# The last scaling of two layer norms, moved from VectorE to ScalarE in thirteen units

## What is computed

```python
x = _layernorm(x + _L0_attn_ref(x, Wqkv, bqkv, Wo, bo))
x = _layernorm(x + _L0_xattn_ref(x, ctx, ctx, Wq, bq, Wk, bk, Wv, bv, gamma, beta))
x = _layernorm(x + _L0_ffn_ref(x, w_router, wi, wo))

def _layernorm(x, axis=-1, eps=1e-05):
    m = jnp.mean(x, axis=axis, keepdims=True)
    v = jnp.var(x, axis=axis, keepdims=True)
    return (x - m) / jnp.sqrt(v + eps)
```

## Time and profile before

| what | value |
|---|---|
| median of 3 runs | 618.51 us (616.61 to 618.95) |
| the profiled execution | 622.54 us |
| its span, first to last instruction | 620.8 us |
| TensorE busy | 516.4 us, 83% |
| VectorE busy | 345.1 us, 56% |
| ScalarE busy | 212.4 us, 34% |
| GpSimd busy | 146.8 us, 24% |
| mean granted TensorE clock | 0.939 |

### The profile page before, as it was taken

How to read it: one execution, slowest core, us unless ns; L and a number is a source line. 1 busy time by engine, 2 the same in 40 slices (tenths; PEclk the granted TensorE clock), 3 DMA queues, 4 the chain that set the end, 5 groups by cost and what they waited for, 6 DMA issues and landing times. The chain is left out here.

```text
span 620.8 us, 12743 instructions
## 1 busy us (share of the span) xinstructions
PE 516.4 (83%) x5028; PEld 400.6 (65%) x5028; DVE 345.1 (56%) x968; ACT 212.4 (34%) x475; POOL 146.8 (24%) x160
## 2 busy tenths in 40 slices
PE   5188696979799989989889879679887999999960
PEld 4156475657567667767667656457677888888850
DVE  3456464646667767777677967674365122243214
ACT  2013253315444544544544624333420110212103
POOL 4000011003004004004104166000213764332330
PEclk9688798979999999999999989799998999999995
DMA  5989917675685585595449566345657734799214
GB/s 167 118 122 140 164 25 124 76 90 69 90 122 92 87 130 86 93 131 79 79 78 148 71 111 187 41 164 172 190 192 256 233 43 54 216 286 277 25 19 139
DMA packets 69383, 77.39 MB, mean 125 GB/s; under 512 B 24094, under 2 KB 62621, under 8 KB 66252
## 3 DMA queue, kind: packets, MB, share of 16 engines
q1 hardware_dynamic: 52456, 37.77, 42.0%
q10 hardware_dynamic: 10724, 33.51, 16.2%
q0 software_dynamic: 6144, 5.29, 5.3%
HBM read 38.74 MB, written 13.74 MB: 85 GB/s over the span
## 5 line engine op out<-in xcount | busy, mean ns | idle before, releaser
L949 DVE TENSOR_REDUCE negm<-nat 128x4 f32<-128x512 f32 (+2 forms) x192 | 120.1, 642 | 86.0 <-PE nat L544 83.3
L768 ACT ACTIVATE probs<-byk 128x512 f32<-128x512 f32 (+1 forms) x192 | 105.5, 564 | 117.2 <-PE byk L544 103.0
L544 PE MATMUL nat<-arena 96*128 96x128 bf16 (+2 forms) x512 | 74.3, 249 | 0.0
L544 PE MATMUL byk<-arena 99*128 99x128 bf16 (+2 forms) x512 | 72.5, 244 | 0.0
L544 PEld LDWEIGHTS nat<-arena 96*128 96x128 bf16 x512 | 47.2, 102 | 16.8 <-issue 3.6
L544 PEld LDWEIGHTS byk<-arena 99*128 99x128 bf16 x512 | 46.2, 100 | 18.1 <-issue 1.4
L540 PE MATMUL nat<-window_q,identb 128*128 128x384 bf16 (+1 forms) x96 | 36.3, 378 | 20.3 <-DMA arena<-parts_k 13.7
L1213 POOL TENSOR_TENSOR resk<-fk,parts_k 128x512 f32<-128x512 f32 x8 | 9.3, 1158 | 160.2 <-ACT fk L709 107.3
L671 PE MATMUL work<-woT,arena 128*128 128x160 f32 x256 | 39.8, 310 | 4.6 <-issue 3.8
L671 PE MATMUL work<-yn_T,arena 128*128 128x160 f32 x256 | 40.6, 313 | 3.4 <-DVE r_s L1124 2.4
L540 PE MATMUL byk<-window_k,identb 128*128 128x384 bf16 (+1 forms) x96 | 34.3, 358 | 10.7 <-DMA arena<-mT 9.9
(11 more groups left out here) (187 smaller groups left out, 887.6 us busy)
## 6 DMA issues: line engine op xcount, KB each, us to landing
arena<-parts_q SPq DMA_DIRECT2D x96, 128.0 KB, 4.8
arena<-parts_k SPq DMA_DIRECT2D x96, 128.0 KB, 5.2
arena<-in_ffn_wi ACTq DMA_DIRECT2D x12, 1024.0 KB, 5.3
arena<-in_ffn_wo ACTq DMA_DIRECT2D x12, 1024.0 KB, 8.7
expert_x<-ranked ACTq DMA_DIRECT2D x4, 650.0 KB, 4.7
xres<-in_x ACTq DMA_DIRECT2D x8, 256.0 KB, 5.7
token_y<-xres SPq DMA_DIRECT2D x8, 256.0 KB, 5.0
xres<-token_y SPq DMA_DIRECT2D x8, 256.0 KB, 3.6
```

The lines of the kernel that those rows point to most:

```text
L544: last = nc.tensor.matmul(bank[:, i * w:(i + 1) * w], lhsT, rhs, start=False, stop=(i == heads - 1), skip_group_check=True)
L768: nc.scalar.activation(dst, src, ACT.Exp, scale=0.25).then_inc(exp_ready, 1)
L949: V.tensor_reduce(dst, src, AX, ALU.max, negate=True).then_inc(nat_free[job % 2], 1)
```

## The change

In the units s0 to s6 and c0 to c5 VectorE stops after the Newton step and one 128x2 instruction, the shift (minus the mean times the root). ScalarE then does both scalings as activations (Identity) with the shift as bias column and the root as scale column. Two new pieces carry them: S3 at 37.9 slots of a self unit (L3 stands at 36.8) and S2 at 38.7 of a cross unit (L2 stands at 37.7). The units s7, c6 and c7 stay as they were. Two waits are added on VectorE, in WO and FQ, so that the rows that ScalarE still reads are not overwritten.

```diff
+SCALED_BY_ACT = {"s": 7, "c": 6}
...
+            if b < SCALED_BY_ACT["s"]:
+                add(n0 + 37.9 - sooner, "S3", k)
...
+            if b < SCALED_BY_ACT["c"]:
+                add(n0 + 38.7, "S2", k)
...
+            def scaled(layer, b, dst_of, ready):
+                act.wait_ge(shifted[layer], b + 1)
+                for t in range(QT):
+                    i = nc.scalar.activation(dst_of(t), r[layer][:, t, :], ACT.Identity, bias=shift[layer][:, t:t + 1], scale=rstd[layer][:, t:t + 1])
+                i.then_inc(ready, 1)
+
+            def S2(k, n, layer, b):
+                scaled("c", b, lambda t: xres[:, b * QT + t, 0:D], x2_ready)
+
+            def S3(k, n, layer, b):
+                scaled("s", b, lambda t: x1[:, b % X1S, t, :], x1_ready)
...
             def FQ(k, n, layer, b):
                 bank = computed(dve, "FQ", k)
                 for name in ("YA", "YB"):
                     emptied(dve, name, k)
+                wait(dve, x2_ready, b)
...
+            def shift_for_act(layer):
+                V.scalar_tensor_tensor(out=shift[layer][:, :], in0=mv[layer][:, :, 0], scalar=-1.0, in1=rstd[layer][:, :], op0=ALU.mult, op1=ALU.mult)\
+                    .then_inc(shifted[layer], 1)
+
...
             def L2(k, n, layer, b):
                 refine("c", 2 * b + 1)
+                if b < SCALED_BY_ACT["c"]:
+                    shift_for_act("c")
+                    return
                 scaled("c", lambda t: xres[:, b * QT + t, 0:D]).then_inc(x2_ready, 1)
 
             def WO(k, n, layer, b):
                 bank = computed(dve, "WO", k)
                 dve.wait_ge(xb_ready, b + 1)
+                wait(dve, x1_ready, b)
...
             def L3(k, n, layer, b):
                 refine("s", b)
+                if b < SCALED_BY_ACT["s"]:
+                    shift_for_act("s")
+                    return
                 scaled("s", lambda t: x1[:, b % X1S, t, :]).then_inc(x1_ready, 1)
```

More of the change, by code:

```diff
@@ L263, in attention_and_experts @@
         newton = sb("newton", [P, QT])
+        shift = {layer: sb(f"shift_{layer}", [P, QT]) for layer in "sc"}
         eps = sb("eps", [P, 1])
@@ L332, in attention_and_experts @@
         x1_ready = sem("x1_ready"); x1b_ready = sem("x1b_ready"); x2_ready = sem("x2_ready")
+        shifted = {layer: sem(f"shifted_{layer}") for layer in "sc"}
         var_ready = {n: sem(f"var_ready_{n}") for n in ("s", "c", "out")}
@@ L869, in _ @@
             walk({"QS": QS, "KS": KS, "KC": KC, "QC": QC, "XC": copy_out("XC", x1_T), "Y2": copy_out("Y2", yn_T, "WO"),
-                  "XR": copy_out("XR", x2_T, "RT"), "MT": MT, "T": T_, "PV": PV, "R1": R1, "R2": R2, "R3": R3, "GC": GC, "XL": XL, "LD": LD, "WL": WL,
+                  "XR": copy_out("XR", x2_T, "RT"), "MT": MT, "T": T_, "PV": PV, "R1": R1, "R2": R2, "R3": R3, "S2": S2, "S3": S3, "GC": GC, "XL": XL, "LD": LD, "WL": WL,
                   "H0": hidden("H0", range(0, 3)), "H2": hidden("H2", range(6, 8)), "FR": FR, "FN": FN})
```

## The result

The changed kernel takes **648.94 us** (median of 4 executions, 642.20 to 652.12) against 618.73 us before: 1.0431 times the time, interval 1.0365 to 1.0497. Measured again, six executions beside 17 of before, it is 646.17 against 621.60, a ratio of 1.0384 [1.0337, 1.0431]. The forecast was 634.4, in a range of 624 to 640. So the direction was right, and the size was too small: 15.9 us were to be added, and 30.2 and 24.6 us were, by these medians. The profiled execution of after took 642.20, the fastest of its four: 19.7 us more than the profiled 622.54 of before.

What follows compares the result with a forecast made beforehand. TensorE, 46.11 of 50 us busy in attention, was taken as the bound. Terms 6.3 + 2.6 + 3.5 - 1.1 + 4.6 = 15.9 us on the median of 618.51 gave 634.4 us, range 624 to 640.

Steps and rivals of the forecast that it cites:

- The sum without the clock: Whole kernel: added waits less the early gain, with no added low-clock stretches, 11.3 us.
- the self units: S3 delays exponentials in s4 to s6, 3.5 us; s1 and s3 gain 1.1 us; s0 and s2 nothing.
- the cross units: S2 on ScalarE delays TensorE: 6.3 us at c0 to c2, 2.6 us at c3 to c5 together.
- the rule weighed there: At c0 to c2: counting the DMA issue at nothing would make each delay 0.9 us less; the prediction counted it.
- The clock: Behind XR's new 2.96 us gaps at c0 to c2, one 1.2 GHz stretch each, 4.6 us; c3 nothing, at most 1.5.
- The early gain of 1.1 us: In s1 and s3 TensorE's waits for VectorE's row maxima and reduction end 0.57 us earlier each, 1.1 us gained.
- The clock stays up: Rival: no low-clock stretches behind the new XR gaps, so 11.3 us added, 629.8 us; chance 0.17.
- A later wait takes it back: Rival: TensorE's 4.74 us wait for the last unit's DMA absorbs up to 4.7 us, 629.7 us; chance 0.13.
- VectorE's relief decides: Rival: S2 and S3 delay nothing and each unit gives back 0.57 us, 7.4 us gained, 611.1 us; chance 0.05.

Runs made afterwards that it cites:

- again: The changed kernel with no edit, run again in six executions beside 17 of the kernel before: 646.17 us, ratio 1.0384 to the kernel before.
- s_only: The changed kernel with only the self units s0 to s6 scaling on ScalarE: 627.05 us, ratio 1.0107 to the kernel before.
- c_only: The changed kernel with only the cross units c0 to c5 scaling on ScalarE: 644.2 us, no interval.
- mt_sp6: The changed kernel with SP instead of ScalarE issuing the row maxima's DMA from unit 6 on: 636.3 us, ratio 1.0235 to the kernel before.
- filler: The changed kernel with TensorE transposing the identity, results unused, while XR of c0 to c3 waits: 637.6 us, ratio 1.0271 to the kernel before.
- s3_late: The changed kernel with only self units scaling on ScalarE, S3 of s4 to s6 behind the exponentials: 619.96 us, ratio 1.0007 to the kernel before.
- s2_first: The changed kernel with S2 at 37.9 slots, ahead of the exponential, maxima's copy and DMA issue: 632.26 us, ratio 1.0187 to the kernel before.
- mended: The changed kernel, all thirteen units, with S2 at 37.9 slots and S3 of s4 to s6 at 40.95: 625.01 us, ratio 1.0086 to the kernel before.

## Why the prediction was right in direction and too low

**Right: the waits.** The sum without the clock was 11.3 us; the rest of again stands 12.4 us above before. That these are so close is in part luck: by s_only and c_only the self units cost 5.3 us in the rest where 2.4 were forecast, and the cross units 8.1 where 8.9 were. At the places themselves the fit is better: XR of c0 to c2 waits for ScalarE's line, 2.89 us against 2.96 forecast; c3's gap is 1.97 against 2.0; the first exponential behind S3 in s4 is 1.44 us late against 1.46. The cause was also right: ScalarE comes to S2 only behind a copy and a DMA issue, and when S2 is put in front of them the gap is 1.24 us. On the rule weighed there, the runs are with the earlier trace rows: taking the issue off ScalarE (mt_sp6) shortened XR's gap by 0.9 us and the kernel by about 9, some of it perhaps not owed to the change. That the issue stops the engine holds for the maxima's, which waits for the copy ahead of it, and not for every issue: in mt_sp6 two others ran beside ScalarE's work. The Trainium skill (DMA: Bandwidth & Descriptors, Issuing engines are not separate DMA queues) calls that issuing time usually small beside the transfer; no run here speaks against the comparison, as after's loads of x take 6.1 us from issue to landing and 0.54 us to issue (medians). But small beside the transfer was not small for the engine that issued.

**Wrong: "The clock", the step "so I take one such stretch for each, 3 x 1.54 = 4.6 us".** That one gap costs one stretch of 3.2 us was read from a single row of before. A gap of the very length that was forecast stood in the same trace, with more than one such stretch behind it:

```profile
132.67 0.50 PE L540 MATMUL byk<-window_k,identb 128*128 128x384 bf16 x1 [2.88 <-DMA arena<-mT]
```

```profile
132.70:138.30 5.60, 5.60 (x24) 4.64 (x25) 2.75 (x6) 0.98 (x2) 1.27 (x1) 0.50 0.25 59
```

In the profile of after, the fastest of its four, it is so: c0, c1 and c2 lose 1.45, 1.59 and 1.60 us. But the same 2.89 us gap is followed in other executions by 6.6 or 10 us at 0.50, and c3's, "nothing" in the prediction, also by a stretch. Take filler's steps at c0 to c3, where the clock stays up, from those of the other profiles: what is left for the clock is 6.2 us in after, 10.7 in again and 12.4 in c_only, where the prediction had 4.6 for the first three and nothing for the fourth. That it is the gap which does it is shown by filler: with ScalarE's delay left as it was, the granted clock behind all four XRs is 1.00 and 7 to 8.5 us are gone by the medians. (The 11.5 us between again and before also hold the low time elsewhere.) This is also why the range was too short at its high end: it held 1.5 us for c3, and nothing for longer stretches.

The rule by which the step chose, one row with the clock down behind 2.51 us and one with it up behind 1.9 us, does not hold in the profiles either, though it gave the right answer for 2.89 us. Behind 2 us the clock fell more often than not, and the row of 2.51 us could as well have shown it up. Of such gaps in all thirteen profiles:

| TensorE's gap | place | followed by 0.50 |
|---|---|---|
| 2.89 to 2.90 us | XR of c0 to c2 | 9 of 9 |
| 2.51 to 2.73 us | Y2 of s7, the place of the earlier trace rows, no filler | 6 of 11 |
| 1.97 to 1.98 us | XR of c0 to c3 | 8 of 11 |
| 1.24 to 1.30 us | XR of c0 to c3 | 1 of 8 |
| 1.10 to 1.14 us | XR of c0 to c3 (filler) | 0 of 4 |
| 0.61 to 0.75 us | XR of c0 to c3 | 0 of 20 |

In after the gap of the earlier trace rows stands so:

```profile
377.35 0.66 PE L491 MATMUL work<-ident,ynat_s 128*128 128x128 f32 x4 [2.52 <-DVEq L1012]
```

```profile
377.40:385.00 7.60, 7.59 (x61) 5.74 (x61) 3.75 (x9) 1.74 (x4) 6.51 (x6) 1.00 0.77 121
```

**Mis-sized: the self units**, 2.4 us net against 5.5 to 6.6 (s_only). s5 and s6 took 1.2 and 1.1 against 1.25 and 1.0. At s4 it was 4.6 against 1.25: the last of the three DMA issues between S3 and the exponential took 2.25 us instead of 0.54 (+1.7), and a slow stretch followed the gap that was left (+1.2). The prediction took the issue's length as unchanged. Why it is long there is open: it was 2.21 in s_only and 0.54 in s3_late, where S3 comes later; in filler it was short at s4, but an issue of 2.1 us stood at s6. One such issue, of 1.8 to 2.25 us, stands at s4, s5 or s6 in six of the seven profiles with S3 at its old place (not in s2_first), and in none of the six others, where the longest is 0.7 us: it goes with S3's place. The slow stretch does not need it: in filler the clock fell at s4 behind a gap of 1.16 us. The early gain of 1.1 us was seen on the spot,

```profile
123.25 0.28 PE L580 MATMUL work<-identb,mp 128*128 128x128 bf16 x2 [0.92 <-DVE mp L979]
```

0.92 in place of 1.75 us, and s3's gap of 0.58 us is gone too, but they were not shown to reach the end: s3_late keeps them and is at 1.0007.

With the measured sizes the sum is 5.3 for the self units and 8.1 for the cross units' waits, 13.4 against a rest of 12.4 in again. For the clock behind XR it is 7 to 8.5 by filler: 20 to 22 us of the 24.6 by the medians of again. The remaining 3 to 4 us are not placed; the slow stretch behind s4 is one candidate.

**The rivals.** "The clock stays up" fell at once, on five stretches at 0.50. "A later wait takes it back" fell too: the wait of 4.74 us for the parts' DMA is still 4.59 us in after, at 409.78. "VectorE's relief decides" was tried in its own terms by s3_late: with nobody delayed, the relief of the self units is worth nothing measurable; for the cross units no kernel without any delay was run. That bears on the Trainium skill's condition for such a move, that VectorE is saturated (Perfetto Trace Analysis, Optimizing Scalar/DVE Operations): with 38.77 us busy of 50 it was not the bound.

**Still open**: why the low clock lasts 3.3 us once and 10 us another time behind equal gaps, why equal gaps of 2.5 and 2.0 us bring it in some executions and not in others, and why one DMA issue is long where S3 stands at its old place. That the longer stretches make up the spread of the executions without a profile is argued from their span and mean clock, not seen in their rows.

## What to carry to other kernels

An instruction given to a less busy engine costs by its place in that engine's order: by what stands in front of it (copies, DMA issues) and by who waits for what comes behind; put it where that engine would wait itself, as s3_late did, and the cost is gone. Where no such place was found, as for S2, a part of it stays (mended, 1.0086). First ask whether the engine relieved is one that TensorE waits for, since otherwise there is nothing to gain. And price an idle gap of TensorE at more than its length, with a spread, when the rows show the lower clock behind such gaps; one row of one execution is not enough, for here equal gaps of 1.3 to 2.5 us went either way. Filling the gaps with useless transposes is then worth a try on the kernel as it stands. Look also for an issue that waits for its own engine's result: what stands behind it waits as well.

## What the hardware showed that was not expected

- Equal gaps, unequal stretches: behind 2.89 us the granted clock was 0.50 for 3.2, 6.6 or 10 us; behind 1.97 us for some 3.4, 6.8 or 10 us or not at all.
- Useless work paid: 220 transposes in nine waits took 0.85% off the kernel before.
- A DMA issue on ScalarE held back what stood behind it when it waited for ScalarE's own copy; without it, two more issues (0.37 and 0.55 us) ran beside a scaling of 128x256, and the exponential behind them was not late (mt_sp6).
- A DMA issue on ScalarE, of one and the same instruction, takes 0.45 to 2.25 us in one execution: 

```profile
L845 ACTq DMA_DIRECT2D xres<-in_x x8: 451/537/2245, 42.2 to 338.9; - x8
```

  (shortest, median and longest in ns).
